# Two layers of attention and gated feed-forward on one core: projection weights that arrive transposed, and a scale found beside the first products

## The reference, cut to what matters

```python
# gate, on h = layernorm(x)
logits = h @ gate_w                              # 8 experts, the top 2 logits are summed
shared = relu(h @ up_w) ** 2 @ down_w            # 512 -> 1024 -> 512
routed = ((h @ fc1_w @ expert_w) * (top1 + top2)) @ fc2_w
g = silu(layernorm(shared + routed) * ln_gamma + ln_beta)

# projections and convolutions, on the same h
qkv = h @ w_qkv.T                                # 1024 of q, 256 of k, 256 of v
v = concat(v_curr, v_prev shifted by one token)
q = conv2(conv1(q))    # conv1: 16 groups of 64 channels, 3 taps; conv2: dense 1024 x 1024, 3 taps
k = conv2(conv1(k))    # the same with 4 groups, 256 channels
q = q + 0.5 * mean of k over its heads;  k = k + 0.5 * mean of q over its heads
# then norms, rotary angles, causal attention, w_o, and layer 1
```

## Time and profile before

| | us |
|---|---|
| median of 3 runs | 2746.51 |
| lowest and highest | 2740.61, 2748.51 |
| the profiled execution: its own time | 2742.68 |
| the profiled execution: its span | 2740.9 |
| PE busy | 2390.5 (87%) |
| DVE busy | 1241.3 (45%) |
| ACT busy | 930.7 (34%) |
| POOL busy | 749.7 (27%) |

### The profile page before, as it was taken

The page is one execution under the profiler, slowest core; times in us unless marked ns, Lnnn a source line. Parts: engine busy times, 40 slices in busy tenths (PEclk is TensorE's granted clock), DMA queues, the critical chain, the costliest instruction groups (busy, mean ns, idle before and its releaser), DMA issues. The chain is left out here.

```text
span 2740.9 us, 45944 instructions
## 1 busy us (share of the span) xinstructions
PE 2390.5 (87%) x19342; PEld 1141.3 (42%) x19342; DVE 1241.3 (45%) x2609; ACT 930.7 (34%) x1616; POOL 749.7 (27%) x749
## 2 busy tenths in 40 slices
PE   7999939999978999999499996898648888888866
PEld 3444424444433444444155552444324444444333
DVE  2332151100143333331267774244568888888712
ACT  1111121001021111110177771122417777777730
POOL 0111011102225222222244441111334434434400
PEclk9999969999989999999799998899869999999988
DMA  6000010010033111000422212331294444444222
GB/s 222 31 31 31 16 69 12 23 35 20 16 121 92 46 39 39 16 16 16 131 91 85 86 59 103 131 125 63 84 183 71 69 70 79 78 77 69 41 98 92
DMA packets 128271, 190.32 MB, mean 69 GB/s; under 512 B 40833, under 2 KB 63105, under 8 KB 126529
## 3 DMA queue, kind: packets, MB, share of 16 engines
q1 hardware_dynamic: 125952, 183.20, 25.6%
q10 hardware_dynamic: 2112, 4.19, 0.4%
HBM read 127.05 MB, written 60.29 MB: 68 GB/s over the span
## 5 line engine op out<-in xcount | busy, mean ns | idle before, releaser
L903 PE MATMUL c_ps_c<-conv_in,c_wT 128*128 128x512 f16 x2304 | 510.9, 382 | 2.5 <-DVE c_wT L1071 2.5
L2329 DVE TENSOR_REDUCE f_chunk_max<-f_ps_a 128x64 f32<-128x1024 f32 x320 | 319.5, 1032 | 63.2 <-PE f_ps_a L2073 40.8
L903 PEld LDWEIGHTS c_ps_c<-conv_in,c_wT 128*128 128x128 f16 x2304 | 223.2, 98 | 281.3 <-issue 16.8
L2200 ACT ACTIVATE f_probs<-f_ps_s 128x512 f32<-128x512 f32 x576 | 305.4, 603 | 99.1 <-PE f_ps_s L2112 46.3
L2073 PE MATMUL f_ps_a<-f_ka,f_qa 128*32 128x512 bf16 (+3 forms) x3072 | 199.6, 339 | 57.7 <-DVE f_chunk_max L2329 25.1
L2104 PE MATMUL f_ps_s<-f_qs,f_ks 128*32 128x512 bf16 x2304 | 208.5, 383 | 23.7 <-ACT f_qs L2191 14.6
L1344 ACT ACTIVATE d_probs<-d_ps_s,d_shift 128x512 f32<-128x512 f32 (+3 forms) x384 | 196.4, 583 | 82.6 <-PE d_ps_s L1283 72.3
L2126 PE MATMUL f_ps_o<-f_probs,f_v 128*32 128x512 f32 (+3 forms) x1536 | 150.7, 490 | 25.8 <-ACT f_probs L2200 25.7
L624 PE MATMUL b_ps<-b_xb,b_wT 128*128 128x512 f32 x320 | 139.9, 597 | 17.9 <-DMA b_xb<-xnT 17.9
L1278 PE MATMUL d_ps_s<-conv_in 128*64 128x512 f16 (+3 forms) x768 | 125.6, 329 | 27.1 <-DMA d_temp<-in_key_temp 27.1
L1294 PE MATMUL d_ps_o<-d_probs,conv_in 128*64 128x512 f32 (+3 forms) x768 | 146.0, 488 | 0.0
(11 more groups left out here) (263 smaller groups left out, 3680.8 us busy)
## 6 DMA issues: line engine op xcount, KB each, us to landing
f_qa<-qk SPq DMA_DIRECT2D x96, 128.0 KB, 3.8
f_qs<-qk SPq DMA_DIRECT2D x96, 128.0 KB, 4.4
conv_in<-q_parts SPq DMA_DIRECT2D x8, 1024.0 KB, 5.3
o0T<-d_stage SPq DMA_DIRECT2D x16, 512.0 KB, 2.6
conv_in<-o0T SPq DMA_DIRECT2D x4, 2048.0 KB, 10.3
qk<-e_part SPq DMA_DIRECT2D x12, 640.0 KB, 4.9
rows<-in_qc_w SPq DMA_DIRECT2D x4, 1536.0 KB, 7.6
c_rows<-in_qc_w SPq DMA_DIRECT2D x4, 1536.0 KB, 8.0
```

The costliest lines, as they stand in the source:

```text
L903: last = pe.matmul(ps_c[n % 2][:], wT[m % 2][:, w, i * TAPS + a, :], conv_in[:, x, i, b, h * CH + a:h * CH + a + CH], start=(i == 0 and a ...
L2200: act.activation(probs[m % HELD][:, :, at:at + P], bank_of["s", i, n][:].rearrange("p (h n) -> p h n", n=P), ACT.Exp, scale=HD1 ** -0.5).t ...
L2329: dve.tensor_reduce(chunk_max[:, qt - 2, :, at:at + w // CHUNK], src.rearrange("p h (c k) -> p h c k", k=CHUNK), AX.X, ALU.max).then_inc(a ...
```

## The change

The host now lays out transposed copies of `w_qkv` and of the first convolutions' weights beside the raw ones (a group's two halves of 64 channels with zeros between), and the kernel loads them ready for use. The block of preparation is gone. `up`, `down` and `x_in` of the gate stage now lie in the space of `conv_in`, and `g_out` in that of `rows0`, so that the projections' weights, biases and token buffers have room beside them. SP issues the weights after the second chunk's tokens, and the first two token loads of the projections before the last store of xnT. What finds the scale is now written into the programs of the projection block: on ACT and DVE ahead of their take-outs, the rest between given units. The sums over heads stand between take-outs of DVE. In the gate stage the statistics of y follow each tile, POOL's fill of the weights' space is a fill of one column, and in the last chunk DVE does gamma and beta of tiles 2 and 3, POOL those of 0 and 1.

```diff
@@ gate_phase @@
-            weights.load(sp)
-            sp.wait_ge(weights.zeroed, 1)
-            weights.load_pairs(sp)
...
             for c in range(NCH - 1):
                 sp.wait_ge(xn_ready, c + 1)
-                sp.dma_start(x_in[:], x_rows[ds(c + 1, 1)].rearrange("a p t d -> p (a t) d")).then_inc(x_loaded, 16)
+                sp.dma_start(x_in, x_rows[ds(c + 1, 1)].rearrange("a p t d -> p (a t) d")).then_inc(x_loaded, 16)
+                if c == 0:
+                    weights.load(sp)
                 store(c)
+            sp.wait_ge(xnT_stored, 16 * 3)
+            sp.wait_ge(weights.x_padded, 1)
+            for h in range(2):
+                weights.load_tokens(sp, 0, h)
             store(NCH - 1)
...
-                    act.wait_ge(shifted, c * TT + t + 1)
+                    if c == NCH - 1 and t >= TT - LAST_DVE:
+                        act.wait_ge(dve_shifted, t - TT + LAST_DVE + 1)
+                    else:
+                        act.wait_ge(shifted, c * TT + t + 1)
                     act.activation(g_out[:, t, :], y[:, t, :], ACT.Silu).then_inc(g_ready, 1)
...
-                for t in range(TT):
+                for t in range(TT if c < NCH - 1 else TT - LAST_DVE):
...
-            pool.memset(weights.pairs, 0.0).then_inc(weights.zeroed, 1)
+            pool.memset(weights.xb[0][:, :, 0:1], 0.0).then_inc(weights.x_padded, 1)
             pool.wait_ge(w2_loaded, 64)
...
                     dve.tensor_tensor(y[:, t, :], y[:, t, :], ps_d[t % 2][:], ALU.add).then_inc(y_ready, 1)
-                for t in range(TT):
                     dve.wait_ge(y_ready, c * TT + t + 3)
                     dve.bn_stats(stats2[:, t, :], y[:, t, :]).then_inc(stats2_done, 1)
...
+                if c == NCH - 1:
+                    for t in range(TT - LAST_DVE, TT):
+                        dve.wait_ge(yn_ready, c * TT + t + 1)
+                        dve.tensor_tensor(y[:, t, :], y[:, t, :], gamma[:], ALU.mult).then_inc(yn_ready, 1)
+                        dve.wait_ge(yn_ready, (c + 1) * TT + t - TT + LAST_DVE + 1)
+                        dve.tensor_tensor(y[:, t, :], y[:, t, :], beta[:], ALU.add).then_inc(dve_shifted, 1)
@@ ProjectionWeights.load, load_tokens @@
+        sp.dma_start(self.wT[:].rearrange("p k o -> p (k o)"), dram["w_qkvT"]).then_inc(self.loaded, 16)
+        sp.dma_start(self.c1T[:].rearrange("p n o -> p (n o)"), dram["qc1_wT"]).then_inc(self.loaded, 16)
+        sp.dma_start(self.kc1T[:].rearrange("p n o -> p (n o)"), dram["kc1_wT"]).then_inc(self.loaded, 16)
+        sp.dma_start(self.kc2T[:].rearrange("p n o -> p (n o)"), dram["kc2_wT"]).then_inc(self.loaded, 16)
+        sp.dma_start(self.rows, dram["w_qkv"][0:LAT].rearrange("(o p) d -> p o d", p=P)).then_inc(self.rows_loaded, 16)
+        sp.dma_start(self.taps, dram["qc1_w"].rearrange("(m p) i a -> p m (i a)", p=P)).then_inc(self.rows_loaded, 16)
+        for name, at, n in (("qc1_b", 0, MQ), ("kc1_b", MQ, MK), ("kc2_b", MQ + MK, MK)):
+            sp.dma_start(self.bias[:, at:at + n], dram[name].rearrange("(m p) -> p m", p=P), allow_slow_non_contiguous=True)\
+              .then_inc(self.rows_loaded, 16)
+
+    def load_tokens(self, sp, b, h):
+        first = b * S + h * CH - h
+        sp.dma_start(self.xb[h][:, :, 1 - h:], self.dram["xnT"].rearrange("k p t -> p k t")[:, :, first:b * S + (h + 1) * CH])\
+          .then_inc(self.x_loaded[h], 16)
@@ project_phase: the block of preparation @@
-                        for j, src in enumerate(blocks):
-                            last = pe.transpose(ps[n % 4][:, j * P:(j + 1) * P], src, ident[:])
...
@@ project_phase: POOL @@
+            pool.memset(k_conv[:, :, 0:PAD], 0.0).then_inc(padded, 1)
+            pool.memset(ones[:], 1.0).then_inc(set_up, 1)
+            pool.memset(root[:, 1:2], 0.5).then_inc(set_up, 1)
+            pool.wait_ge(set_up, 2)
+            pool.wait_ge(bound_step, 5)
+            pool.tensor_tensor(root[:, 0:1], most_all[:, 0:1], root[:, 1:2], ALU.pow).then_inc(rooted, 1)
             pool.memset(conv_in[:, :, :, :, 0:PAD], 0.0)
-            pool.memset(xb[0][:, :, 0:1], 0.0).then_inc(padded, 1)
@@ PE @@
-            pe.wait_ge(padded, 1)
+            pe.wait_ge(weights.loaded, 64)
...
+                        if b == h == 0 and u == 4:
+                            find_peaks()
+                        if b == h == 0 and u == 6:
+                            share_peaks()
@@ take, units 10 to 17 @@
+                if n == 0 and u < C0 + 2:
+                    engine.wait_ge(bound_step, BOUND_STEPS)
@@ ACT, ahead of its take-outs @@
+            act.wait_ge(weights.rows_loaded, 16 * 5)
+            for x in range(PIECES):
+                tiles = slice(x * PER, (x + 1) * PER)
+                act.activation(taps[:, tiles, :], taps[:, tiles, :], ACT.Abs)
+                act.activation(size[:, tiles], bias[:, tiles], ACT.Abs)
+                act.activation(rows[:, tiles, :], rows[:, tiles, :], ACT.Square).then_inc(measured, 1)
@@ DVE @@
+            dve.wait_ge(weights.loaded, 64)
+            measure()
             for b in range(B):
                 for h in range(2):
                     for u in range(1, UNITS, 2):
                         take(dve, b, h, u).then_inc(took_dve, 1)
+                        if b == h == 0:
+                            if u == 3:
+                                highest()
+                            elif u == 5:
+                                spread()
+                            elif u == 7:
+                                bound()
+                            elif u == 9:
+                                for k in range(KD):
+                                    sum_heads(0, k)
+                            elif u in (11, 13):
+                                for k in range(2):
+                                    sum_heads(1, u - 11 + k)
+                            elif u == 15:
+                                means()
```

More of the change, by code:

```diff
@@ L346, with __init__, sb @@
 class ProjectionWeights:
-    def __init__(self, dram, sem, space):
+    def __init__(self, ctx, dram, nc, sem, space, rows0):
+        def sb(name, shape):
+            return ctx.enter_context(nc.sbuf_tensor(f"b_{name}", shape, F32))
         flat = space[:].rearrange("p a m b n -> p (a m b n)").bitcast(F32)
-        NO = (LAT + 2 * KVD) // P
-        ends = [NO * D, (MQ + MK) * P * TAPS, MK * KVD * TAPS]
-        at = [sum(ends[:i]) for i in range(4)]
+        ends = [MQ * D, MQ * HD0 * TAPS, KD * INT, MI * D, TT * D]
+        at = [sum(ends[:i]) for i in range(len(ends) + 1)]
@@ L367, in load_pairs @@
[L367 to L373, removed]
+        dram = self.dram
+        sp.dma_start(self.wT[:].rearrange("p k o -> p (k o)"), dram["w_qkvT"]).then_inc(self.loaded, 16)
@@ L529, in project_phase @@
-        xb = [sb(f"xb{i}", [P, KD, CH + 1]) for i in range(2)]
+        sums = sb("sums", [P, 2, MQ])
+        most = sb("most", [P, 3])
+        most_all = sb("most_all", [P, 3])
+        peak = sb("peak", [3, 1])
+        peaks = sb("peaks", [3, 3])
+        ones = sb("ones", [3, P])
+        root = sb("root", [P, 2])
+        size = sb("size", [P, MQ])
+        ps_w = ctx.enter_context(nc.psum_tensor("b_ps_w", [P, P], F32))
+        measured = sem("b_measured")
+        set_up = sem("b_set_up")
@@ L542, in project_phase @@
         low_ready = sem("b_low_ready")
-        x_loaded = [sem(f"b_x_loaded{i}") for i in range(2)]
         made = sem("b_made")
@@ L614, in _, with find_peaks, share_peaks @@
         def _(pe):
-            pe.wait_ge(padded, 1)
+            pe.wait_ge(weights.loaded, 64)
+            def find_peaks():
+                pe.wait_ge(bound_step, 2)
+                pe.matmul(ps_w[0:3, :], most[:], ident[:], start=True, stop=True).then_inc(peak_done, 1)
+            def share_peaks():
+                pe.wait_ge(bound_step, 4)
+                pe.wait_ge(set_up, 2)
+                pe.matmul(ps_w[:, 0:3], ones[:], peaks[:], start=True, stop=True).then_inc(peak_done, 1)
             def unit(b, h, u):
@@ L698, in _, with measure @@
             primed(dve, took_dve, N_DVE)
+            def measure():
+                for x in range(PIECES):
+                    tiles = slice(x * PER, (x + 1) * PER)
+                    dve.wait_ge(measured, x + 1)
+                    dve.tensor_reduce(sums[:, 0, tiles], rows[:, tiles, :], AX.X, ALU.add)
+                    last = dve.tensor_reduce(sums[:, 1, tiles], taps[:, tiles, :], AX.X, ALU.add)
+                last.then_inc(bound_step, 1)
+                dve.wait_ge(bound_step, 1)
+                dve.tensor_reduce(most[:, 0:2], sums[:], AX.X, ALU.max)
+                dve.tensor_reduce(most[:, 2:3], size[:], AX.X, ALU.max).then_inc(bound_step, 1)
@@ new lines, in sum_heads, with means @@
+            def sum_heads(n, k):
+                at, heads = ((LAT, KV0), (0, H0))[n]
+                dve.tensor_reduce(mean[:, n, k, :], wT[:, k, at:at + heads * HD0].rearrange("p (h c) -> p c h", c=HD0),
```

(17 more changed lines are left out.)

207 lines of the change are left out of this document (58 added, 149 removed).

## The result

The changed kernel takes 2701.98 us (median of 4, 2701.53 to 2705.39), the kernel before 2745.18 (4 runs, 2740.61 to 2748.51): ratio 0.9846, 95% interval 0.9829 to 0.9863, 43.2 us between the medians. The forecast was 2700. The profiled execution took 2701.93 us with a span of 2700.1, 40.8 less than before. PE is busy for 2379.7 us, 88% of it.

A forecast was written before the change was run, and what follows sets the result against it. It took PE's 60 us standstill between gate and projection stages as the target: -37.9 + 0.8 - 4.9 - 1.0 - 1.8 = -44.8 us, giving 2697.9 from the profile or 2701.7 from the median; forecast 2700, range 2689 to 2712.

The forecast's parts named there:

- the dips: Gate stage: expert products at lowered clock, 1.7 us per affected chunk; two chunks now, none to four after, +-3.4 us.
- the cold start: Start of projections: PE at 1.2 GHz after idling, taken as unchanged; about 1.9 us of cold clock.
- The serial 37.9 us: Between gate and projection stages: removing preparation and token load saves 37.9 us, bounds 36 to 38.5.
- +0.8 us: First projection units: two pairs of tiny scale products add 0.8 us on PE, bounds 0.5 to 3.
- The tail: End of gate stage: statistics per tile and gamma/beta shared by DVE and POOL save 4.9 us (3 to 5.8).
- The start and the hole: Gate stage: smaller POOL fill saves 1.0 us at its start; earlier second-chunk tokens remove PE's 1.79 us wait near 46.8.
- the cover of 40 us: Gate stage: first xnT store, queued behind weights until about 46 us, is not needed by ACT until about 95.
- The sums over heads: First projection chunk: DVE sums fit between take-outs at cost 0; without cover, at most 5 us.
- A: First projection chunk: late sums, scale or tokens give part back; gain 20 to 38 us, 2708 to 2726; 12%.
- C: Projection stage: PE stays at 1.2 GHz, making the kernel slower, 2790 us over two chunks; 2%.
- D: Projection stage start: PE still waits for weights or tokens; 2738 us if all 38 us stay; 2% for within 0.3%.
- B: Gate stage: no clock drops, earlier PE start and full gain at its end; gain 51 us, 2694; beyond that 3%.

The follow-up runs named there:

- the added 22 us: Changed kernel with each of the four wide sums over heads done four times, three into spare space: 2716.54 us.

## Why the prediction was right

**How near it was.** The sum was 44.8 us against the profiled execution, whose span fell by 40.8; the medians are 43.2 apart. So the sum was 4.0 us too high against the trace. The forecast lay 2 us from the measured median in part because it was put between the sum's two results, 2697.9 and 2701.7. Most of the 4.0 is in terms that differ between executions of the same work: the dips (1.7), the cold start (0.8) and the stages behind the projections (1.5).

**The serial 37.9 us.** Right, and now split: 9 us for the chain of the scale and 5 for the tokens are shown by undoing them; the 24 that remain are transposes, copies and sums over heads by subtraction, and no run undid them alone. About 10 of them are the sums and their scaling, by their place in the earlier trace rows.

**The cold start and the small products.** The step that said "the cold start the same" and "+0.8 us" was short by 1.0. Each pair of small products cost 0.5, which shows at the take-outs of units 5 and 7: 22.6 and 29.4 us behind the first product before, 23.9 and 31.2 after, against 8.8 and 9.6 at unit 1. The other 0.8 is there from the first unit on, and it is the clock. These are windows of PE before and then after, as in the earlier trace rows:

```profile
404.00:408.00 4.00, 4.00 (x9) 0.73 1.04 426
```

```profile
360.00:364.00 4.00, 4.00 (x6) 0.54 0.83 338
364.00:368.00 4.00, 4.00 (x11) 1.00 0.04 18
```

The level is either 0.50 or 1.00, so a mean of 0.73 puts the rise at 406.2, 3.4 us after PE's first product, and not 5 us as the prediction read from the window behind; a mean of 0.54 puts it at 363.7, 5.0 us after the first product. The difference of 1.6 us at half the clock is the 0.8. Seven more traces in which the same ten units follow a pause of PE give 2.9 to 5.9 us, so that this start was the longer one is chance, as with the dips. Its price in the changed kernel is 2.5 us by the run with PE kept busy; the text reckoned 1.9.

**The tail.** The sum was right, its inside wrong in one place. I let the meeting of DVE and POOL lengthen POOL's products by 0.4 each, as in the earlier trace rows. It lengthened mostly DVE's: 1.75 and 1.64 us for products of 0.69, beside POOL's at 1.44 and 1.59, which take 1.44 and 1.26 where POOL does all four tiles. So POOL was done at 351.3 and DVE only at 353.1, and the last Silu waited for DVE, not for three tiles in a row behind POOL as the sum had it. The two errors nearly cancel: the tail gave 4.6 us, not 4.9, and that the sum fits so well is partly luck. The rule cited from the Trainium skill (SBUF — State Buffer, Who interferes with whom) spoke of contention and is borne out: two DVE products took about as long as the POOL product beside them. It did not cost what full exclusion of all four would have, for POOL was done after two of DVE's four products.

**The start and the hole.** 1.1 and 2.2 us where 1.0 and 1.8 were forecast. PE's releaser at 14.21 is the expert load, as was said. That the hole hangs on the tokens' place in the queue is shown by the run that puts them behind the weights. Landing was forecast at 20 to 25 us and was 24.5. The store of the first xnT is issued at 44 us, after 18 us in which SP sat on one issue of biases; the cover of 40 us held.

**The sums over heads.** Cost 0, as forecast, though DVE needed 1.93 us a sum beside POOL on average, not 1.86. The four scalings behind them took more than twice their time, 0.90 us before and 2.21 beside POOL's casts, and that too was covered:

```profile
413.04 2.21 DVE L671 TENSOR_SCALAR b_meanT<-b_mean 128x256 f32<-128x256 f32 x4
```

The slack was taken for about 10 us in the expectation; the added 22 us cost 10.4 of standing still, so it was about 12.

**The dips.** A dip is a stretch at 1.2 GHz in or behind the logits. They were left open as +-3.4. In this trace the first chunk's dip came earlier, within the logits, and cost 3.4 instead of 1.7, so the head's gain of 3.3 ended as 1.7. Where a dip falls differs between executions of kernels with the same gate stage; it is the term that a forecast can only bound.

**The rivals.** A did not happen: PE shows no wait in the first projection chunk. C did not: PE had its full clock from 363.7 us to the end of that chunk. D did not: PE's first product comes with the stage's first instructions. B's gain of 51 us was not reached; the dips took 1.7 us instead of giving 3.4. Of the signs of being wrong one came up by its letter, a later stage longer by more than 3 us: the last stretch is 3.7 longer. It says nothing against the account, since that stretch differs by up to 5.8 us between the twelve traces.

## What to carry to other kernels

A block of preparation between two stages can be priced by the first instruction that it delays and the first that it frees, and its parts by undoing each. What remains in such a gap afterwards is worth a look of its own: here the wait for a store that only one later load needed, and a chain over four tiles of which three could be done beside PE, gave 11 us more by the rows (7.0 and 3.9). And the place of one load in an issue queue decides whether it comes before or behind all that its queue holds, 14 us here.

## What the runs showed of the hardware

When a DVE product with two inputs in SBUF meets a POOL product, either may be the slower one: 0.72 and 1.72 us in the earlier trace rows, 1.75 and 1.44 in the changed kernel. In both it was the one that began later, by 0.13 and 0.24 us. SP's issue of a load of single elements took 18.0 us when it came behind 8.4 MB of loads, in a stretch in which the queue moved some 420 GB/s, and all that SP had to issue next was late by as much. In the run with the weights ahead of the tokens the long issue was the one just before it, 15.0 us. TensorE's clock fell to 1.2 GHz within or behind 32 narrow instructions although the engine shows as fully busy (0.50 granted from 60 to 62 us of the changed kernel, with PE busy all of the time), in 21 of 44 chunks, and behind an idle gap of 7 us.
